# Attention and a four-layer gated FFN on one core: the operand differences of the two square layers go from GpSimd to VectorE, and the order of the work around them changes

## The chip, the cores and the metric

One core of a Trainium2 chip runs the whole kernel. The metric is the device time of one execution in microseconds, as the median over several runs; a run's profile is one execution more, with a time of its own.

## The reference, cut to what matters

H has 16 batches of 512 tokens by 256 features. Each is normalised; the result feeds a linear attention with 16 heads and a gated FFN with two square hidden layers of 1024, and all of it is added up.

```
xn  = layernorm(x)
# attention
q, k, v = split(xn @ W_qkv.T + b_qkv);  q, k = elu(q)+1, elu(k)+1
o   = (q @ (k.T @ v)) / clip(q . sum(k), 1e-6)          # per head
att = layernorm(o @ W_proj.T + b_proj) * gamma + beta + xn
# FFN, _tlin(x, w, s) = (x @ w.T) * s, w ternary
h   = silu(_tlin(xn, w1, s1)) * _tlin(xn, w2, s2)
h   = gelu(_tlin(h, h1, s))        # square, 1024 x 1024
h   = gelu(_tlin(h, h2, s))        # square, 1024 x 1024
out = x + att + _tlin(h, w3, s3)
```

## The kernel before, in words

A tile is one batch: 512 tokens. The loop runs over 16 tiles; the first has a body of its own (plain products, while the weights arrive), the next 14 are a loop, the last a copy of it without a successor. Each engine has one program, in order, written out by hand; engines meet at semaphores, which count named steps (`Count`, `Named`). A `Named` counter takes its value from the place of a name in a tuple, so the tuples `HI`, `LO` and `POOL_T` fix the order in which ScalarE, VectorE and GpSimd make their blocks.

The stages of a tile on PE are: eight gate groups (`gate_group`), with the attention's small products between them; the first square layer; the second square layer; the output groups with the projections of q, k and v of the next tile between them. The gate groups use a ring of three pairs of PSUM banks, so group n waits until VectorE has made the gated value of group n-3 (`gated`). The attention of this tile ends inside the first square layer: `to_rows` (transposes) and `proj_step`.

A square layer is computed by a scheme of seven products instead of eight (Winograd's form of Strassen). The operand's four blocks are B11, B12, B21, B22 (halves of the features by halves of the tokens), and the differences are T1 = B12-B11, T2 = B22-T1, T3 = B22-B12, T4 = B21-T2. Product i takes the block `X_OF[i]`: 1 B11, 5 T1, 6 T2, 7 T3, 2 B21, 3 B22, 4 T4, in this order. Output features are cut in four sets: sets 0 and 1 are the first layer, 2 and 3 the second; a step of `products(t, pair, i, parts)` computes product i of both sets of a layer. The operand of the first layer is in two groups G0 and G1, that of the second in H0 and H1.

Each operand is split for precision: `hi_of_block` and `hi_of_difference` on ScalarE write the high part as float32r, `lo` on VectorE (L1713) writes value x 4096 minus high as float16. A product takes the high parts and the low parts in two passes; `HI_FIRST` and `LO_FIRST` say which pass is first. The weights are ternary and exact in one part.

The partial sums of a layer are made by VectorE from the banks (`add_u`, `add_w`, `add_c22`, `add_c12`, `add_c21`, all L1739); `product_bank_read` is the wait of a product until its bank has been read. ScalarE applies the gelu (`gelu_of`).

GpSimd computes the differences (`t1` L756, `t2` L763, `t3` L768, `t4` L773), the roots of both LayerNorms (`inverse_root`, L746), and issues the refills of the weight ring. The ring holds seven blocks in four parts (`RING_PARTS`), and is filled four times a tile from DRAM (`refill`, L783): `refill(t, turn, g)` waits until the last product that reads part g in this turn is done, then loads that part for the next turn. SyncE loads the next x, stores the output, and loads six pieces of raw weights a tile (`load_piece`, L599), which VectorE inspects for bits that a shortened form would lose (`check_piece`, L1828); piece j+1 is requested when piece j has been inspected.

At the end of a tile VectorE adds gain, shift and sum of the attention's LayerNorm (`ln2_gain_and_shift`, `ln2_sum`), makes the low parts of the output operand (`lo_of_output`, L1720), reads the projections of the next tile (`z_step`, `phi_q`, `phi_k`) and writes the output halves (`output`). PE's `kv_step(t, c)` for c of 2 and 3 reuses the bank that `z_step(t, c-2)` has read.

Of the kernel before, what the change touches and what calls it, by code (L numbers as in the profile page):

```python
# [9 lines left out]
ALU = mybir.AluOpType  # L10
# [139 lines left out]
      "H0B11", "H1B11", "H0T1", "H1T1", "H0T2", "H1T2", "H0T3", "H1T3", "H0B22", "H1B22", "H0T4", "H1T4", "H0B21", "H1B21",  # L150
# [28 lines left out]
def block_kernel(nc, H, w_ffn, w_attn, vecs, rows, consts, out):  # L179
# [233 lines left out]
    pool_t = Named(sem("difference_made_by_pool"), POOL_T)  # L413
# [77 lines left out]
    def difference_made(t, group, block):  # L491
        return pool_t.after(t, group + block)
# [78 lines left out]
    with block:  # L571
# [163 lines left out]
        def _(pool):  # L735
# [18 lines left out]
            def t1(t, group):  # L754
                pool.wait_ge(*value_made(t, group, "B12"))
                tt(value(group, "T1"), value(group, "B12"), value(group, "B11"), ALU.subtract).then_inc(pool_t.sem, 1)  # L756

            def t2(t, group):
                pool.wait_ge(*value_made(t, group, "B22"))
                pool.wait_ge(*difference_made(t, group, "T1"))  # L760
                if group == "H1":
                    pool.wait_ge(*prod.after(t, "1P4"))
                tt(value(group, "T2"), value(group, "B22"), value(group, "T1"), ALU.subtract).then_inc(pool_t.sem, 1)  # L763

            def t3(t, group):
                pool.wait_ge(*value_made(t, group, "B22"))
                pool.wait_ge(*difference_made(t, group, "T1"))
                tt(value(group, "T3"), value(group, "B22"), value(group, "B12"), ALU.subtract).then_inc(pool_t.sem, 1)  # L768

            def t4(t, group):  # L770
                pool.wait_ge(*value_made(t, group, "B21"))
                pool.wait_ge(*lo_made(t, group, "T2"))
                tt(value(group, "T4"), value(group, "B21"), value(group, "T2"), ALU.subtract).then_inc(pool_t.sem, 1)  # L773

# [52 lines left out]
            def body_of(first):  # L827

                def body(t, more):
                    filling = first == 0  # L830
                    t1(t, "G0")
                    t2(t, "G0")
                    t4(t, "G0")
                    t3(t, "G0")
# [8 lines left out]
                    if filling:  # L843
                        refill(t, 0, 1)
                        refill(t, 0, 2)
# [1356 lines left out]
```

## Time and profile before

| | us |
|---|---|
| median of 3 runs | 1586.86 (1582.5 to 1591.64) |
| the profiled execution | 1580.62 |
| its span | 1578.7 |
| PE busy | 1485.9 (94%) |
| VectorE (DVE) busy | 1237.4 (78%) |
| ScalarE (ACT) busy | 927.2 (59%) |
| GpSimd (POOL) busy | 513.4 (33%) |
| DMA | 287.67 MB, 182 GB/s in the mean |

The profile is of one execution. Busy time is summed over an engine's instructions; PE's weight loads (PEld) overlap its matmuls. The first 126 us hold the first tile, then the same pattern of stages repeats tile after tile. Where an engine stood idle, the views name what released it.

### The profile page before, as it was taken

What the parts mean: (1) busy time and instruction counts of PE and PEld (TensorE: products, weight loads), DVE (VectorE), ACT (ScalarE), POOL (GpSimd) and SP (SyncE); (2) the same over time, 40 slices, a digit from 0 to 9 for tenths busy, and PEclk for the clock granted to TensorE, in tenths of its full rate; (3) what the DMA queues carried; (4) which work ended last, traced back from release to release, by engine and by line L of the source; (5) the groups of instructions that cost most, each with busy time, mean ns of one, the idle gap of its engine ahead of it and who ended that gap; (6) DMA issues with size and microseconds to landing.
All of it is one profiled execution on the core that took longest, in us unless ns stands there. A gap on an engine that the chain in (4) does not pass through costs nothing.

```text
span 1578.7 us, 33322 instructions
## 1 busy us (share of the span) xinstructions
PE 1485.9 (94%) x11020; PEld 1284.1 (81%) x11020; DVE 1237.4 (78%) x2088; ACT 927.2 (59%) x1727; POOL 513.4 (33%) x584
## 2 busy tenths in 40 slices
PE   9999999999999999999999998999999999999998
PEld 6998878788787887878878788788887878878887
DVE  6857878779687786877978779687786878968778
ACT  4545656556565565655666556565556656656564
POOL 2203415134151341513425034250342404424142
PEclk9999999999999999999999999999999999999999
DMA  8796726537165371653727438174481743817444
GB/s 234 232 318 214 280 70 223 199 102 282 62 222 200 103 280 64 224 198 117 263 67 252 170 132 287 39 251 160 132 285 44 256 159 129 287 39 263 152 146 151
DMA packets 89091, 287.67 MB, mean 182 GB/s; under 512 B 9696, under 2 KB 55392, under 8 KB 65760
## 3 DMA queue, kind: packets, MB, share of 16 engines
q0 software_dynamic: 43296, 231.75, 42.8%
q1 hardware_dynamic: 44928, 54.29, 10.5%
q10 hardware_dynamic: 832, 1.18, 0.2%
q8 instruction: 19, 0.31, 0.1%
q14 instruction: 16, 0.13, 0.0%
HBM read 270.42 MB, written 25.17 MB: 187 GB/s over the span
## 4 chain that ended last, share of the span: by engine, by line
PE 40%; issue 19%; DVE 14%; ACT 11%; POOL 8%; DMA 6%; DVEq 1%; POOLq 0%; ACTq 0%; SPq 0%
PE ps L1018 7%; PE ps L1016 6%; PE ps L1045 6%; DMA raw_weights<-weight_blocks 4%; PE ps L905 4%; PE ps L1132 4%; PE ps L1080 4%; PE ps L907 3%; PE ps L906 3%; DVE lo_a_in_bits L1713 3%; ACT values_out L1384 3%; POOL values_a L768 2%; DVE lo_b_in_bits L1713 2%; PE ps L957 2%; DVE attention_by_row L1693 2%
## 5 line engine op out<-in xcount | busy, mean ns | idle before, releaser
L1045 PE MATMUL ps<-operands_a,hidden_weights 128*128 128x256 f32 x2520 | 353.8, 284 | 0.0
L1045 PE MATMUL ps<-lo_a_in_bits,hidden_weights 128*128 128x256 f16 x2520 | 320.8, 273 | 0.0
L1045 PEld LDWEIGHTS ps<-operands_a,hidden_weights 128*128 128x128 f32 x2520 | 319.6, 189 | 0.5
L1045 PEld LDWEIGHTS ps<-lo_a_in_bits,hidden_weights 128*128 128x128 bf16 x2520 | 242.3, 98 | 30.0
L1713 DVE SCALAR_TENSOR_TENSOR lo_a_in_bits<-values_a,operands_a 128x512 f16<-128x512 f32 x315 | 231.4, 758 | 29.7 <-ACT operands_a L1356 18.3
L783 POOL DMA_DIRECT2D hidden_weights<-weight_blocks x236 | 131.8, 559 | 337.0 <-PE ps L1045 301.1
L756 POOL TENSOR_TENSOR values_a<-values_a 128x512 f32<-128x512 f32 x45 | 57.9, 1288 | 399.1 <-DVE values_a L1704 380.1
L1045 PE MATMUL ps<-operands_b,hidden_weights 128*128 128x256 f32 x840 | 140.1, 289 | 48.0 <-DMA hidden_weights<-weight_blocks 24.1
L1713 DVE SCALAR_TENSOR_TENSOR lo_b_in_bits<-values_b,operands_b 128x512 f16<-128x512 f32 x105 | 167.2, 1592 | 6.8 <-ACT operands_b L1356 6.4
L1045 PEld LDWEIGHTS ps<-operands_b,hidden_weights 128*128 128x128 f32 x840 | 114.0, 189 | 54.6 <-issue 51.8
L1356 ACT ACTIVATE operands_a<-values_a 128x512 fp32r<-128x512 f32 x180 | 113.3, 629 | 67.2 <-POOL values_a L756 26.5
L1018 PE MATMUL ps<-xnT,w_ffn 128*128 128x512 f32 x512 | 150.5, 421 | 0.0
L1648 DVE TENSOR_TENSOR zkv<-ps,row_vectors 128x512 f32<-128x512 f32 x64 | 44.2, 691 | 117.1 <-PE ps L907 116.9
L1739 DVE TENSOR_TENSOR partial_sums<-partial_sums,ps 128x512 f32<-128x512 f32 x150 | 102.3, 682 | 36.8 <-PE ps L1045 36.7
L1045 PE MATMUL ps<-lo_b_in_bits,hidden_weights 128*128 128x256 f16 x840 | 128.0, 275 | 0.1
L1310 ACT ACTIVATE gate_ring<-ps,vectors 128x512 f32<-128x512 f32 x128 | 86.1, 684 | 67.0 <-PE ps L1016 47.6
L1016 PE MATMUL ps<-xnT_lo_in_bits,w_ffn 128*128 128x512 f16 x512 | 124.6, 381 | 0.0
L1384 ACT ACTIVATE values_out<-partial_sums,vectors 128x256 f32<-128x256 f32 x90 | 40.9, 502 | 137.5 <-DVE partial_sums L1739 137.5
L1384 ACT ACTIVATE values_b<-partial_sums,vectors 128x256 f32<-128x256 f32 x90 | 40.8, 501 | 133.0 <-DVE partial_sums L1739 133.0
L1704 DVE SCALAR_TENSOR_TENSOR values_a<-ps,vectors,gate_ring 128x512 f32<-128x512 f32 x128 | 94.1, 745 | 30.0 <-ACT gate_ring L1310 29.9
L1018 PEld LDWEIGHTS ps<-xnT,w_ffn 128*128 128x128 f32 x512 | 93.1, 189 | 21.2
L1402 ACT ACTIVATE exp_tmp<-zkv 128x256 f32<-128x256 f32 x64 | 26.6, 416 | 123.6 <-DVE q L1642 67.2
(167 smaller groups left out, 2965.1 us busy)
## 6 DMA issues: line engine op xcount, KB each, us to landing
hidden_weights<-weight_blocks POOLq DMA_DIRECT2D x180, 1024.0 KB, 5.5
hidden_weights<-weight_blocks POOLq DMA_DIRECT2D x60, 512.0 KB, 5.1
raw_weights<-weight_blocks SPq DMA_DIRECT2D x70, 231.5 KB, 3.0
hidden_weights<-in_w_ffn POOLq DMA_DIRECT2D x16, 512.0 KB, 7.9
weight_blocks<-weight_sums SPq DMA_DIRECT2D x16, 512.0 KB, 4.8
weight_blocks<-in_w_ffn SPq DMA_DIRECT2D x16, 512.0 KB, 10.1
out_dram<-acc SPq DMA_DIRECT2D x31, 256.0 KB, 2.2
x<-in_H SPq DMA_DIRECT2D x15, 512.0 KB, 5.4
```

Of the source, the lines that this page charges most:

```text
L783: pool.dma_start(of_ring(ring, g), part_weights((turn + 1) % SETS, g)).then_inc(ring_loaded[g].sem, 16)
L905: mm(bank, wl, xh, start=first, stop=False)
L1016: r = mm(gate_bank(o, j), high_halves(wk), xnT_short[:, k, :], start=begins, stop=ends)
L1018: r = mm(gate_bank(o, j), wk, as_used(xnT[:, k, part, :]), start=begins, stop=ends)
L1045: r = mm(bank[:, m * HT:(m + 1) * HT], wk, xk, start=i in firsts and begins and m == 0 and j == 0, stop=i in lasts and ends and m == 1 and ...
L1080: r = mm(bank[:, m * HT:(m + 1) * HT], wk, parts[part][:, j, :], start=n < 4 and g == 0 and part == order[0] and m == 0 and j == 0, stop=n ...
L1310: nc.scalar.activation(gate[:, n % 2, :], gate_bank(o, 0), ACT.Silu, scale=vec[:, V_GATE + o:V_GATE + o + 1]).then_inc(silu_made.sem, 1)
L1356: nc.scalar.activation(hi_part(group, block), value(group, block), ACT.Copy, scale=LIFT).then_inc(hi.sem, 1)
L1384: r = nc.scalar.activation(dst, src[:, m * HT:(m + 1) * HT], ACT.Gelu, scale=vec[:, col:col + 1])
L1704: v.scalar_tensor_tensor(out=ha_values[:, o % HK, first:first + 2, 1, :], in0=two(gate_bank(o, 1)), scalar=vec[:, V_UP + o:V_UP + o + 1], ...
L1713: v.scalar_tensor_tensor(out=part, in0=value(group, block), scalar=LIFT, in1=hi_part(group, block).bitcast(F32), op0=ALU.mult, op1=ALU.sub ...
L1739: v.tensor_tensor(partial(s, dst), partial(s, kept), product_bank(s, i), ALU.add).then_inc(add.sem, 1)
```

## The change: what it does

The eight differences of each layer are computed by VectorE (`difference`, with `t1` to `t4` in its program), each once, with the same operands; the counter is renamed. GpSimd's program keeps the roots and the refills. Three refills more stand ahead of the LayerNorm 1 root (the four of turn 0, then parts 0 and 1 of turn 1), three between the roots (turn 1's parts 2 and 3, turn 2's part 0), and turn 2's part 1 stands behind the LayerNorm 2 root.

The orders change too. On PE the third product of the first layer runs before the row transposes, the fourth before the projection, and some steps swap their passes. On VectorE the sums of the first layer come before the rows' low part, `ln1_stats` and `ln2_stats` later, and in tiles with a successor `ln2_gain_and_shift` and `ln2_sum` move from before the first output block to behind the last. On ScalarE the exponentials of q go ahead of each last high part, and `residual` ahead of G1's T3.

```diff
@@ tuples
-POOL_T = ("G0T1", "G0T2", "G0T4", "G0T3", "G1T1", "G1T2", "G1T3", "G1T4",
-          "H0T1", "H1T1", "H0T2", "H1T2", "H0T3", "H1T3", "H0T4", "H1T4")
+DVE_T = ("G0T1", "G0T2", "G0T3", "G0T4", "G1T1", "G1T2", "G1T3", "G1T4", "H0T1", "H1T1", "H0T2", "H1T2", "H0T3", "H1T3", "H0T4", "H1T4")
@@ GpSimd, body: all t1..t4 removed, the rest in this order
                     if filling:
                         refill(t, 0, 0)
                         refill(t, 0, 1)
                         refill(t, 0, 2)
+                        refill(t, 0, 3)
+                        refill(t, 1, 0)
+                        refill(t, 1, 1)
                     if more:
                         ln1(t + 1)
                     if filling:
-                        refill(t, 0, 3)
-                        refill(t, 1, 0)
+                        refill(t, 1, 2)
+                        refill(t, 1, 3)
+                        refill(t, 2, 0)
                     inverse_root(t, 1, ln2_var, ln2_root)
                     if filling:
...
                         refill(t, 2, 1)
@@ PE, body
                     products(t, 0, 5, LO_FIRST)
+                    products(t, 0, 6, HI_FIRST)
                     to_rows(t, 0)
                     to_rows(t, 1)
-                    products(t, 0, 6, HI_FIRST)
+                    products(t, 0, 7, HI_FIRST)
                     proj_step(t, 0)
                     proj_step(t, 1)
-                    products(t, 0, 7, HI_FIRST)
-                    products(t, 0, 2, LO_FIRST)
-                    products(t, 0, 3, HI_FIRST)
-                    products(t, 0, 4, LO_FIRST)
-
-                    products(t, 1, 1, HI_FIRST)
-                    products(t, 1, 5, LO_FIRST)
-                    products(t, 1, 6, HI_FIRST)
+                    products(t, 0, 2, HI_FIRST)
+                    products(t, 0, 3, LO_FIRST)
+                    products(t, 0, 4, HI_FIRST)
+
+                    products(t, 1, 1, LO_FIRST)
+                    products(t, 1, 5, HI_FIRST)
+                    products(t, 1, 6, LO_FIRST)
@@ ScalarE, body
                 keep_first(t, 1)
+                residual(t)
                 hi_of_difference(t, "G1", "T3")
-                residual(t)
...
                 gelu_of(t, 3, "C21")
+                if more:
+                    q_act(t + 1, 0)
                 hi_of_output(t, 0, "C21")
+                if more:
+                    q_act(t + 1, 1)
                 hi_of_output(t, 1, "C21")
@@ VectorE
+            def difference(t, group, block, one, other):
+                v.tensor_tensor(value(group, block), value(group, one), value(group, other),
+                                ALU.subtract).then_inc(dve_t.sem, 1)
+            def t2(t, group):
+                if group == "H1":
+                    dve.wait_ge(*prod.after(t, "1P4"))
+                if group[0] == "G":
+                    dve.wait_ge(*value_made(t, group, "B22"))
+                dve.wait_ge(*difference_made(t, group, "T1"))
+                difference(t, group, "T2", "B22", "T1")
@@ VectorE, body, gate stage
                     cut_kv(t, 1)
+                    t1(t, "G0")
                     lo(t, "G0", "B11", first > 0)
+                    gated(t, 5)
                     lo(t, "G0", "T1", first > 0)
-                    gated(t, 5)
+                    t2(t, "G0")
                     normalise(t, 0)
                     gated(t, 2)
+                    t3(t, "G0")
                     lo(t, "G0", "T2", first > 0)
                     gated(t, 6)
+                    t4(t, "G0")
                     swap(t, 0)
                     gated(t, 3)
+                    t1(t, "G1")
                     lo(t, "G1", "B11", first > 0)
                     gated(t, 7)
+                    lo(t, "G1", "T1", first > 0)
+                    t2(t, "G1")
                     normalise(t, 1)
-                    lo(t, "G1", "T1", first > 0)
                     lo(t, "G0", "T3", first > 0)
                     lo(t, "G1", "T2", first > 0)
                     swap(t, 1)
+                    t3(t, "G1")
+                    t4(t, "G1")
@@ VectorE, body, second layer
                     add_c12(t, 0)
                     add_c12(t, 1)
+                    t1(t, "H0")
+                    t1(t, "H1")
+                    t2(t, "H0")
                     add_c21(t, 0)
                     add_c21(t, 1)
+                    t2(t, "H1")
 
                     lo(t, "H0", "T1", first > 0)
                     lo(t, "H1", "T1", first > 0)
                     lo(t, "H0", "T2", first > 0)
                     lo(t, "H1", "T2", first > 0)
+                    t3(t, "H0")
+                    t3(t, "H1")
+                    lo(t, "H0", "B22", first > 0)
+                    lo(t, "H1", "B22", first > 0)
+                    ln2_stats(t)
+                    lo(t, "H0", "T3", first > 0)
+                    lo(t, "H1", "T3", first > 0)
+                    add_u(t, 2)
+                    add_u(t, 3)
+                    t4(t, "H0")
+                    t4(t, "H1")
                     if checking and more:
                         check_piece(t - 1, 1)
@@ VectorE, body, end of the tile
-                    ln2_gain_and_shift(t)
-                    ln2_sum(t)
+                    if not more:
+                        ln2_gain_and_shift(t)
+                        ln2_sum(t)
...
                     lo_of_output(t, 0, "C21", first > 0)
                     lo_of_output(t, 1, "C21", first > 0)
                     if more:
+                        ln2_gain_and_shift(t)
+                        ln2_sum(t)
                         z_step(t + 1, 0)
                         output(t, 0)
```

## Rows read from the trace of the kernel before

**Rows 1.** The page, parts 1 and 2: busy time, granted clock in 40 slices.
```profile
PE 1485.9 (94%) x11020; PEld 1284.1 (81%) x11020; DVE 1237.4 (78%) x2088; ACT 927.2 (59%) x1727; POOL 513.4 (33%) x584
...
PEclk9999999999999999999999999999999999999999
```

**Rows 2.** Waits of PE, 810 to 907: total us, times, longest.
```profile
PE ps L905 <- ACT relu_tmp L1397: 1.8, 1, 1.8
PE ps L1045 <- DVE partial_sums L1739: 1.7, 1, 1.7
PE ps L1045 <- DMA hidden_weights<-weight_blocks: 1.7, 1, 1.7
PE ps L905 <- DVE attention_by_row L1693: 0.5, 1, 0.5
PE ps L1132 <- ACT hidden_out L1361: 0.4, 1, 0.4
```

**Rows 3.** Stages of one tile: us, busy us of each engine, clock, DMA, GB/s.
```profile
806.00:824.00 18.00, 18.00 (x97) 12.31 (x96) 13.78 (x29) 11.23 (x19) 5.10 (x4) 1.00 0.09 28
...
854.00:867.00 13.00, 11.28 (x99) 10.52 (x98) 12.60 (x8) 9.96 (x20) 11.38 (x12) 1.00 0.90 334
...
884.00:903.00 19.00, 16.81 (x106) 13.92 (x105) 12.12 (x21) 10.79 (x22) 0.53 (x1) 1.00 0.37 126
```

**Rows 4.** Timeline of DVE, 850 to 870: start, us, instruction, idle before.
```profile
855.16 4.09 DVE L1713 SCALAR_TENSOR_TENSOR lo_b_in_bits<-values_b,operands_b 128x512 f16<-128x512 f32 x1
...
859.77 3.53 DVE L1713 SCALAR_TENSOR_TENSOR lo_b_in_bits<-values_b,operands_b 128x512 f16<-128x512 f32 x1
...
863.83 1.78 DVE L1828 SCALAR_TENSOR_TENSOR low_bits<-raw_weights,low_bits 128x463 uint32<-128x463 uint32 x1
865.53 1.76 DVE L1713 SCALAR_TENSOR_TENSOR lo_b_in_bits<-values_b,operands_b 128x512 f16<-128x512 f32 x1
```

**Rows 5.** Timeline of POOL, 840 to 867.
```profile
840.93 1.04 POOL L746 TENSOR_TENSOR rstd<-var_plus_eps,power 128x4 f32<-128x4 f32 x1 [4.52 <-DVE minus_mean L1597]
...
849.81 1.43 POOL L746 TENSOR_TENSOR rstd<-var_plus_eps,power 128x4 f32<-128x4 f32 x1 [5.32 <-DVE minus_mean L1597]
...
851.90 1.15 POOL L783 DMA_DIRECT2D hidden_weights<-weight_blocks  x2 [0.38 <-issue]
...
857.40 1.29 POOL L763 TENSOR_TENSOR values_a<-values_a 128x512 f32<-128x512 f32 x1
...
865.04 1.70 POOL L773 TENSOR_TENSOR values_a<-values_a 128x512 f32<-128x512 f32 x1
```

**Rows 6.** Groups of DVE by form: count, busy us, mean ns, idle before.
```profile
L1797 DVE TENSOR_TENSOR acc<-acc,partial_sums 128x512 f32<-128x512 f32 x31 | 21.5, 693 | 2.3
...
L1777 DVE TENSOR_TENSOR projected<-projected,row_vectors 128x1024 f32<-128x1024 f32 x16 | 19.5, 1219 | 0.0
```

**Rows 7.** Timeline of DVE, gate stage.
```profile
815.21 0.29 DVE L1664 TENSOR_TENSOR kv_by_head<-ps,constants 128x128 f32<-128x128 f32 x1 [1.14 <-PE ps L957]
...
822.36 0.75 DVE L1704 SCALAR_TENSOR_TENSOR values_a<-ps,vectors,gate_ring 128x512 f32<-128x512 f32 x1 [0.32 <-ACT gate_ring L1310]
```

**Rows 8.** Timeline of ACT at the end of the gate stage.
```profile
823.15 0.63 ACT L1343 ACTIVATE operands_a<-values_a 128x512 fp32r<-128x512 f32 x1 [0.30 <-DVE values_a L1704]
```

**Rows 9.** Timeline of PE, products of both square layers and the next gate stage.
```profile
824.01 2.13 PE L1045 MATMUL ps<-operands_a,hidden_weights 128*128 128x256 f32 x16
...
841.42 3.67 PE L1045 MATMUL ps<-lo_a_in_bits,hidden_weights 128*128 128x256 f16 x32
...
869.82 0.74 PE L1045 MATMUL ps<-operands_b,hidden_weights 128*128 128x256 f32 x4 [1.75 <-DVE partial_sums L1739]
...
903.14 1.10 PE L1018 MATMUL ps<-xnT,w_ffn 128*128 128x512 f32 x4
```

**Rows 10.** Landing of the check pieces, 806 to 904 (line L599).
```profile
DMA to landing us min/median/max: 1.7/2.8/5.3
```

**Rows 11.** Landing of the ring's refills, whole span (line L783).
```profile
DMA to landing us min/median/max: 3.4/5.2/8.1
```

More of the change, by code:

```diff
@@ L491, in difference_made @@
     def difference_made(t, group, block):
-        return pool_t.after(t, group + block)
+        return dve_t.after(t, group + block)
     def value_made(t, group, block):
@@ L1734, in plain_lo_of_output, with t1, t3, t4 @@
                                        op1=ALU.subtract).then_inc(plain_lo.sem, 1)
+            def difference(t, group, block, one, other):
+                v.tensor_tensor(value(group, block), value(group, one), value(group, other),
+                                ALU.subtract).then_inc(dve_t.sem, 1)
+            def t1(t, group):
+                dve.wait_ge(*value_made(t, group, "B12"))
+                difference(t, group, "T1", "B12", "B11")
+            def t2(t, group):
[5 more added lines that the diff above has]
+                difference(t, group, "T2", "B22", "T1")
+            def t3(t, group):
+                dve.wait_ge(*difference_made(t, group, "T1"))
+                difference(t, group, "T3", "B22", "B12")
+            def t4(t, group):
+                dve.wait_ge(*value_made(t, group, "B21"))
+                dve.wait_ge(*lo_made(t, group, "T2"))
+                difference(t, group, "T4", "B21", "T2")
             def sum_into(t, s, i, dst, kept):
@@ L2049, in body @@
                     lo(t, "G1", "B21", first > 0)
+                    add_u(t, 0)
+                    add_u(t, 1)
                     rows_lo(t, 0)
                     rows_lo(t, 1)
-                    add_u(t, 0)
-                    add_u(t, 1)
                     lo(t, "G0", "B22", first > 0)
                     lo(t, "G1", "B22", first > 0)
-                    if more:
-                        ln1_stats(t + 1)
                     add_w(t, 0)
@@ L2063, in body @@
                     lo(t, "G1", "T4", first > 0)
-                    ln2_stats(t)
+                    if more:
+                        ln1_stats(t + 1)
+                    lo(t, "H0", "B11", first > 0)
+                    lo(t, "H1", "B11", first > 0)
                     if checking and more:
@@ L2068, in body @@
                     add_c12(t, 1)
-                    lo(t, "H0", "B11", first > 0)
-                    lo(t, "H1", "B11", first > 0)
+                    t1(t, "H0")
+                    t1(t, "H1")
+                    t2(t, "H0")
                     add_c21(t, 0)
                     add_c21(t, 1)
+                    t2(t, "H1")
                     lo(t, "H0", "T1", first > 0)
@@ L2113, in body @@
                     lo_of_output(t, 1, "C11", first > 0)
+                    lo_of_output(t, 0, "C12", first > 0)
+                    lo_of_output(t, 1, "C12", first > 0)
                     add_c21(t, 2)
                     add_c21(t, 3)
-                    lo_of_output(t, 0, "C12", first > 0)
-                    lo_of_output(t, 1, "C12", first > 0)
                     if checking and more:
```

56 lines of the change are left out of this document (2 added, 54 removed).

## The prediction

> **What bounds the kernel now.** The page first: PE is busy 94% of the span at the full clock, so PE can only be given back its waits [rows 1]. Its timeline repeats every 97.1 us, once a tile. I take the tile whose gate groups begin at 806.0; its successor's begin at 903.14 [rows 9]. PE's waits in it are five and add up to 6.1 us: 0.5 for the projection's rows, 1.7 for a refill, 1.7 for VectorE's sums, 0.4 for the output operand, 1.8 for q's exponentials [rows 2]. Then the stages: in 854 to 867 VectorE is busy 12.60 of 13 us and GpSimd 11.38; in the gate stage and in the tail both have room [rows 3]. The timelines of the two say why. Three low halves of H0 take 4.09, 3.53 and 1.76 us and a check piece 1.78, where the usual is 0.68 and 0.64, and the first ends 0.5 us after a pair of GpSimd subtractions does (858.69), the last 0.5 us after one that ends at 866.74 [rows 4, 5]. The excess is 3.4+2.85+1.1+1.1 = 8.5 us a tile. The 1.7 us until 869.82 is this backlog: product 7 waits for the sum of set 2 [rows 9]. The 1.7 us for the DMA begins at GpSimd: it sits in the LayerNorm 2 root until 851.5 and only then, at 851.90, issues the refill of part 1, freed at 846.8; it lands 5.1 us later [rows 5].
>
> The Trainium skill (SBUF — State Buffer, Who interferes with whom) says that a VectorE instruction with two SBUF inputs and a GpSimd instruction that reads SBUF exclude each other, the second waiting for the first. By that rule too the stretch goes with the subtractions.
>
> **The change part by part,** on that tile's clock.
>
> *The subtractions.* 16 leave GpSimd (1.29 us each) and join VectorE. This form is not on VectorE now; the nearest rows are 512 columns from two SBUF tiles in 0.69 us and 1024 in 1.22, so 512 more columns cost 0.53 and an instruction in a row about 0.60 [rows 6]. I take 0.60, 9.6 us a tile (bounds 0.53 and 0.69: 8.5 to 11). The removed stretch is 8.5 (bounds 0, if it stays, and 8.5). VectorE's total stays near 79 us a period; what counts is where the work stands.
>
> *Gate stage (six of them before the products).* VectorE has gaps up to 815.2. From there chained: cut 0.35, T1 0.6, low B11 0.6, gated 5 0.65, low T1 0.6, T2 0.6, normalisation 1.7, gated 2 0.65, T3 0.6, low T2 0.6, gated 6 0.65, T4 0.6, swap 0.7: 8.9 us, so gated 3 starts at 824.1, not 822.36 [rows 7]. G1's first high half on ScalarE, at 823.15 now, comes at 824.9 to 825.5 [rows 8]. Product 1 starts at 824.01 and needs it after its first quarter of 0.5 us [rows 9]: **a new PE wait of 1.1**. The gate groups' banks are free in time (gated 2 ends at 821.0, the last group starts at 821.2: 0.2 of slack). Later in this layer: low T1 of G1 is made at 828.0 and wanted at 829.3, low T2 at 831.5 and 834.5, the rows' low part at 839.8, before the projection at 840.8, because product 7 now runs ahead of it: the 0.5 wait goes. The layer with projection ends at 854.7 (now 854.1).
>
> *Refill wait.* Part 1 of turn 1 is issued ahead of the roots, when product 2 ends at 847.4, and lands at 852.7: the 1.7 goes. Its cover is 2 us; were GpSimd held up by more, it would return.
>
> *Second layer.* VectorE: sums C12 at 852.7 (product 3 ends at 851.0), ScalarE's gelu of C12 853.0 and 853.8, T1s 853.7 and 854.5, T2 of H0 855.1, sums C21 856.3, T2 of H1 856.9, low T1s 858.1, low T2s 859.4 (on ScalarE's high halves), T3s 860.6, low B22s 861.8, LayerNorm 2 statistics 3.3 us to 865.1, low T3s 866.3, sum of set 2 866.9. PE has products 1, 5, 6 without a wait, 3 times 3.67, and the transposes 0.9: 854.7 to 866.6 [rows 9]. **Wait 0.4** for the sum, where 1.7 was. But the root now stands before the refill of part 1, turn 2: statistics 865.1, issue 2.2 later (as 849.7 to 851.9), landing 5.1 later: 872.4 [rows 5, 11]. PE wants it at 870.7: **a new wait of 1.7** (bounds 0 and 4.6, from the landings of 3.4 and 8.1). Still product 2 starts 1.2 ahead of its 873.6 now. Behind it stands the check: piece 1 is inspected at 869.3, not 865.6, so piece 2 is asked for with three refills in flight and lands after 2.8 to 5.3 us [rows 10]. VectorE waits there, in order, until 872.6 or 874.9, and behind it stand the sums that free product 3's bank: **0 to 1.2**. I take half, 0.6. The products end at 883.9 (now 884.5).
>
> *Tail.* q's exponentials go ahead of a high half: the 1.8 shrinks to 0.2, and out_group's 0.4 goes, its operand being a microsecond ahead. But the last low half comes 1.3 us later in ScalarE's row (the second half's exponentials lie before it), and behind it VectorE has gain, shift and sum, 3 times 1.22 and gaps, 3.75 us [rows 6], before the first z. Chained: last low half 893.6, sum 897.4, z0 898.0, output 899.5, z1 900.1. PE wants z0 at 897.7 and z1 at 899.4: **0.3 and 0.7**. The next gate stage starts at 901.8 (bounds 901.3 and 902.2 by the piece's landing): 1.3 us a tile, 0.9 to 1.8. The balance says the same: 6.1 leave; 1.1+0.4+1.7+0.6+0.2+0.3+0.7 = 5.0 come; between 1.1 and 1.3.
>
> *At nothing.* The swapped passes leave the number of changes between float32 and float16 matmuls as it is. ln1_stats stands 6 us later; its root is wanted at 861 and done by 850. residual ahead of G1's T3: that high half is made at 834.0, wanted at 837.6. No SyncE instruction moves; the output's store still has 24 us until residual.
>
> **Sum.** 14 tiles with a successor at 1.3, the last 0.8: 19 us. The profiled execution took 1580.6 us (span 1578.7 and 1.9 around it): 1561.6. The median of the three runs is 1586.9, 0.4% above that execution; 1586.9-19 = 1568, say 1567.
>
> The same section of the Trainium skill (SBUF — State Buffer) speaks against the change too: GpSimd's roots read SBUF, and VectorE's many two-input instructions may hold them off. The power took 1.04 us in one place and 1.43 in the other [rows 5], so this case shows 0.4. By the rule each of the roots' short instructions could wait for one of VectorE's, 0.6; the sum would be at most 1.2 us a tile worse, 17 in all.
>
> **Rivals.**
> A, more (chance 0.21): the piece lands in 2.8 us, the refill in 3.4. 2.5 to 3.5 us a tile: 1535 to 1550. For it: SyncE's pieces land in under 3 us as a rule. Against: three refills in flight.
> B, nothing (0.16): 1579 to 1594. Five new waits hang on one in-order VectorE; a quarter microsecond more in each eats the 1.3.
> C, slower (0.16): the turn of the tile is bound by VectorE. z, output, phi and gated 0 stand in one row behind the 3.75 us; each microsecond by which that row is later than I have it moves kv_step, the gate stage and G1's high half one for one. It decides from 1.3 us a tile; at 2.5 the price is 1.2 x 15 = 18: 1605. For it: there is nothing in the row to drop. Against: VectorE is busy 12.12 of 19 us in that tail [rows 3].
> D, the stretch comes from the refills' issue, not the subtractions (0.03): 8.5 stays and 4.8 of subtractions come on top in the second layer; PE waits 4 us a tile more: 1645. Against: two refills are issued between 873 and 875 and nothing is stretched there.
> The forecast has 0.44, with an own range of 1555 to 1579.
>
> 0.5% (8 us) is what a measurement of this kernel can tell from no change. Faster 0.44+0.21 = 0.65, same 0.16, slower 0.16+0.03 = 0.19. The range 1538 to 1597 leaves out A's best end, D and C's far part.
>
> **What would show it.** Low halves of H0 at 0.68 us throughout; VectorE's busy time within 20 us of 1237, GpSimd's down by some 300; no DMA wait at the second layer's first product, one of about 1.7 at its product 2; about 1.1 for ScalarE's high half in the first product; two below 1 at kv_step; a period near 95.8. Wrong if the halves stay stretched, if PE waits in the gate groups, or if the period is over 96.7.

## The result, and the profile after

The changed kernel takes 1604.95 us (median, 1602.9 to 1606.0) against 1588.3 for the kernel before: ratio 1.0103, 95% interval 1.008 to 1.0125. It is slower by 1%, where I forecast 1567 and gave "slower" 0.19. The profiled execution took 1602.9 us, 22 more than that of before.

The page of the changed kernel, parts 1 and 2:

```profile
PE 1494.5 (93%) x11020; PEld 1290.0 (81%) x11020; DVE 1243.2 (78%) x2328; ACT 925.1 (58%) x1727; POOL 207.7 (13%) x344
...
PEclk9999999999999999999999999999999999999999
```

VectorE's busy time is within 6 us of what it was, as forecast, and GpSimd's fell by 306 us [rows 1]. The stretch is gone: groups by form of the changed kernel, the low halves of H0 and the subtractions (count, busy us, mean ns, idle before).

```profile
L1695 DVE TENSOR_TENSOR values_a<-values_a 128x512 f32<-128x512 f32 x180 | 121.4, 681 | 2.1
...
L1670 DVE SCALAR_TENSOR_TENSOR lo_b_in_bits<-values_b,operands_b 128x512 f16<-128x512 f32 x105 | 71.9, 684 | 43.1 <-ACT operands_b L1298 43.0
```

0.684 us where the mean was 1.59. A subtraction takes 0.68 by itself and its successor starts 0.60 us later, which is the cost that I took. So the idea of the change works, and the time is lost elsewhere. Who PE waits for in one tile of the changed kernel, 813 to 912 (total us, times, longest), the rows that answer to [rows 2]:

```profile
PE ps L1000 <- DVE partial_sums L1723: 4.0, 2, 3.6
PE ps L1000 <- DMA hidden_weights<-weight_blocks: 1.7, 1, 1.7
PE ps L1000 <- ACT operands_a L1298: 0.6, 1, 0.6
PE ps L860 <- ACT relu_tmp L1352: 0.6, 1, 0.6
PE ps L860 <- DVE zkv L1605: 0.5, 2, 0.4
```

7.4 us instead of 6.1. Each is one that the prediction named; one has another size. The timeline of PE in that tile:

```profile
874.52 0.74 PE L1000 MATMUL ps<-operands_b,hidden_weights 128*128 128x256 f32 x4 [0.47 <-DVE partial_sums L1723]
...
880.10 0.61 PE L1000 MATMUL ps<-lo_b_in_bits,hidden_weights 128*128 128x256 f16 x4 [1.66 <-DMA hidden_weights<-weight_blocks]
...
887.47 0.74 PE L1000 MATMUL ps<-operands_b,hidden_weights 128*128 128x256 f32 x4 [3.56 <-DVE partial_sums L1723]
...
902.13 0.50 PE L860 MATMUL ps<-wqkv_parts,xnT 128*128 128x512 f32 x1 [0.56 <-ACT relu_tmp L1352]
...
909.41 0.50 PE L860 MATMUL ps<-wqkv_parts,xnT 128*128 128x512 f32 x1 [0.17 <-DVE zkv L1605]
...
911.42 0.50 PE L860 MATMUL ps<-wqkv_parts,xnT 128*128 128x512 f32 x1 [0.35 <-DVE zkv L1605]
...
912.92 1.10 PE L973 MATMUL ps<-xnT,w_ffn 128*128 128x512 f32 x4
```

0.47 for the sum of set 2 (forecast 0.4), 1.66 for the refill behind the root (1.7), 0.56 for the exponentials (0.2), 0.17 and 0.35 for z (0.3 and 0.7), and at the first product 0.59 for ScalarE's high half (1.1). And 3.56 us at product 3, where I had 0.6. The tile starts at 813.79 and the next at 912.92: 99.1 us, where I said 95.8 and 97.1 was. (Of the 2.0 us more only 1.3 stand in these rows. Most of the other 0.7 shows when starts are compared instead of idle times: each wait puts the next start off by 0.16 to 0.24 us more than its row says, there are seven waits in place of five, and one of 0.2 at 903.84 has no row.) What VectorE does ahead of the sums that PE waits for, its timeline:

```profile
876.11 0.63 DVE L1812 SCALAR_TENSOR_TENSOR low_bits<-raw_weights,low_bits 128x463 uint32<-128x463 uint32 x1
...
884.31 0.64 DVE L1812 SCALAR_TENSOR_TENSOR low_bits<-raw_weights,low_bits 128x463 uint32<-128x463 uint32 x1 [4.56 <-DMA raw_weights<-weight_blocks]
884.86 0.68 DVE L1587 SCALAR_TENSOR_TENSOR xnT<-ps,xnT 128x512 fp32r<-128x512 f32 x1
885.47 0.68 DVE L1723 TENSOR_TENSOR partial_sums<-partial_sums,ps 128x512 f32<-128x512 f32 x1
```

It stands 4.56 us in front of check piece 2. Four sums follow (885.47 to 887.9), and the third of them frees PE's bank. GpSimd and SyncE say why the piece is late, their timelines:

```profile
857.16 0.74 POOL L747 TENSOR_TENSOR minus_mean_by_rstd<-minus_mean,rstd 128x4 f32<-128x4 f32 x1
...
872.68 1.40 POOL L745 TENSOR_TENSOR rstd<-var_plus_eps,power 128x4 f32<-128x4 f32 x1 [6.65 <-DVE minus_mean L1554]
874.16 0.20 POOL L747 TENSOR_TENSOR minus_mean_by_rstd<-minus_mean,rstd 128x4 f32<-128x4 f32 x1
874.74 1.15 POOL L761 DMA_DIRECT2D hidden_weights<-weight_blocks  x2 [0.38 <-issue]
878.14 0.53 POOL L761 DMA_DIRECT2D hidden_weights<-weight_blocks  x1 [2.25 <-PE ps L1000]
879.04 0.53 POOL L761 DMA_DIRECT2D hidden_weights<-weight_blocks  x1 [0.37 <-issue]
```

```profile
876.90 0.34 SPq L598 DMA_DIRECT2D raw_weights<-weight_blocks  x1
```

The LayerNorm 2 root ends at 874.4 and lets two refills go at once, two more follow at 878.14 and 879.04, 3.5 MB in all. Piece 2 is asked for at 876.90 in the middle of them and lands after 7.3 us, at 884.21. The four refills land at 879.9, 882.7, 885.5 and 886.7, so the piece lands behind the two that were asked for before it and ahead of the two behind it. The landings over six tiles, first of the kernel before, then of the changed one (line of the check pieces):

```profile
DMA to landing us min/median/max: 1.5/2.7/5.7
```

```profile
DMA to landing us min/median/max: 1.8/2.6/7.4
```

One thing more is in the records: the granted clock of PE. It stands at one of two levels, full (2.4 GHz) or half (1.2 GHz); a stretch at half, which lasts 3.4 or 6.8 us here, is called a fall below. Its mean over the profiled execution is 0.983 where it was 0.989. That is a difference between two executions and not between the kernels: over their executions the changed kernel shows 0.979 to 0.983, and the kernel before 0.977 to 0.984 in the 26 that ran beside e1 to e8.

### The profile page after: what moved, and what is told of

Its sections match the earlier page's. It is cut to its first block, busy times and chain, and to the rows that moved or that the text cites. A ratio compares the mean times of both kernels' runs of the same rounds, so it can differ in the third digit from the quotient of the medians.

```text
span 1601.1 us, 33162 instructions
## 1 busy us (share of the span) xinstructions
PE 1494.5 (93%) x11020; PEld 1290.0 (81%) x11020; DVE 1243.2 (78%) x2328; ACT 925.1 (58%) x1727; POOL 207.7 (13%) x344
## 4 chain that ended last, share of the span: by engine, by line
PE 43%; DVE 22%; issue 12%; ACT 11%; DMA 10%; DVEq 2%; SPq 0%; ACTq 0%
PE ps L1000 20%; DMA raw_weights<-weight_blocks 10%; PE ps L973 4%; PE ps L971 4%; PE ps L1035 3%; DVE partial_sums L1723 3%; ACT values_a L1339 3%; DVE values_a L1695 3%; DVE lo_a_in_bits L1670 2%; PE ps L860 2%; PE ps L862 2%; PE ps L861 2%; ACT values_out L1339 2%; PE ps L912 2%; PE ps L1087 2%
## 5 line engine op out<-in xcount | busy, mean ns | idle before, releaser
L1000 PE MATMUL ps<-operands_a,hidden_weights 128*128 128x256 f32 x2520 | 361.0, 287 | 8.9 <-ACT operands_a L1298 8.9
L1000 PEld LDWEIGHTS ps<-operands_a,hidden_weights 128*128 128x128 f32 x2520 | 327.7, 193 | 12.3 <-ACT operands_a L1298 12.0
L1670 DVE SCALAR_TENSOR_TENSOR lo_a_in_bits<-values_a,operands_a 128x512 f16<-128x512 f32 x315 | 209.0, 683 | 13.5 <-ACT operands_a L1311 13.5
L1000 PE MATMUL ps<-operands_b,hidden_weights 128*128 128x256 f32 x840 | 150.2, 303 | 58.5 <-DVE partial_sums L1723 58.5
L1000 PEld LDWEIGHTS ps<-operands_b,hidden_weights 128*128 128x128 f32 x840 | 121.0, 201 | 65.4 <-issue 61.0
L1677 DVE SCALAR_TENSOR_TENSOR lo_out_in_bits<-values_out,hidden_out 128x512 f16<-128x512 f32 x120 | 78.6, 687 | 78.8 <-ACT hidden_out L1316 78.8
L1812 DVE SCALAR_TENSOR_TENSOR low_bits<-raw_weights,low_bits 128x463 uint32<-128x463 uint32 x84 | 53.3, 634 | 98.9 <-DMA raw_weights<-weight_blocks 98.9
L1695 DVE TENSOR_TENSOR values_a<-values_a 128x512 f32<-128x512 f32 x180 | 121.4, 681 | 2.1
L1000 PEld LDWEIGHTS ps<-lo_b_in_bits,hidden_weights 128*128 128x128 bf16 x840 | 79.5, 101 | 39.9 <-DVE lo_a_in_bits L1670 15.3
L1670 DVE SCALAR_TENSOR_TENSOR lo_b_in_bits<-values_b,operands_b 128x512 f16<-128x512 f32 x105 | 71.9, 684 | 43.1 <-ACT operands_b L1298 43.0
```

Source lines behind the costliest of these rows:

```text
L1000: r = mm(bank[:, m * HT:(m + 1) * HT], wk, xk, start=i in firsts and begins and m == 0 and j == 0, stop=i in lasts and ends and m == 1 and ...
L1670: v.scalar_tensor_tensor(out=part, in0=value(group, block), scalar=LIFT, in1=hi_part(group, block).bitcast(F32), op0=ALU.mult, op1=ALU.sub ...
L1677: v.scalar_tensor_tensor(out=part, in0=hg_values[p][:, :, O_SLOT[c], 1, :], scalar=LIFT, in1=hg[p][:, :, O_SLOT[c], 0, :].bitcast(F32), op ...
L1695: v.tensor_tensor(value(group, block), value(group, one), value(group, other), ALU.subtract).then_inc(dve_t.sem, 1)
```

## The experiments

The *period* below is the mean distance, over 14 tiles of the profiled execution, between ScalarE's loads of the silu table, one a tile: 97.85 us before, 99.37 after. "Clock" is the mean granted clock of PE in the profiled execution.

| kernel | median us | ratio to before (95%) | period | clock |
|---|---|---|---|---|
| before | 1588 to 1591 | 1 | 97.85 | 0.989 |
| changed | 1604.95 | 1.0103 (1.008 to 1.0125) | 99.37 | 0.983 |
| e1 check early | 1542.96 | 0.9695 (0.9679 to 0.9711) | 95.09 | 0.998 |
| e2 refill early | 1542.27 | 0.9692 (0.9676 to 0.9709) | 95.03 | 0.998 |
| e3 both | 1531.0 | 0.9625 (0.9609 to 0.9641) | 94.18 | 0.999 |
| e4 piece 2 behind the sums | 1600.95 | 1.0068 (1.0051 to 1.0085) | 99.16 | 0.988 |
| e5 no pieces | 1526.88 | 0.9604 (0.9585 to 0.9623) | 93.94 | 1.000 |
| e6 before, check late | 1591.3 | 1.0012 (0.9997 to 1.0027) | 98.67 | 0.984 |
| e7 e3, differences on GpSimd | 1570.85 | 0.9881 (0.9861 to 0.99) | 97.49 | 0.991 |
| e8 e3, ballast | 1594.56 | 1.0035 (1.0024 to 1.0046) | 99.07 | 0.970 |
| e9 tuned | 1507.97 | 0.9505 (0.9474 to 0.9535) | 92.68 | 1.000 |
| e10 before, root later | 1586.77 | 0.9993 (0.9974 to 1.0012) | 98.44 | 0.975 |

**e1_check_early.**

```diff
                     lo(t, "H1", "T2", first > 0)
+                    if checking and more:
+                        check_piece(t - 1, 1)
                     t3(t, "H0")
...
                     t4(t, "H1")
-                    if checking and more:
-                        check_piece(t - 1, 1)
```

> One edit to the changed kernel: VectorE inspects raw piece 1 right after the low T2s of the second layer (where the kernel before had it), not after both T4s. Theory Q (queue): the changed kernel is slow because piece 2 is asked for some 8 us later than before, at the moment when the LayerNorm 2 root has let four refills go at once; it lands 7.3 us later and VectorE stands in front of the sums that free product 3's bank (PE's 3.56 us). Asked for 7 us earlier it lands before the backlog: that PE wait goes, period 99.1 to about 95.6, time 1602.9 - 14 x 3.5 = 1554 (1550 to 1565). Rival L (load): the sums are late because VectorE now carries 16 subtractions; then the wait only changes its name and under 1 us a tile comes back: 1590 to 1603.

Measured: 1543, 62 us faster than the changed kernel and 7 below the low end of what I expected. One instruction of VectorE's row for a tile moved up, and nothing else. Piece 2 is now asked for 9.2 us earlier in the tile and lands in about 3 us. (The expectation has the changed kernel ask for it 8 us later than the kernel before; in the tiles shown it is 3.3.) PE's waits in one of its tiles, 780 to 875:

```profile
PE ps L1000 <- DMA hidden_weights<-weight_blocks: 1.6, 1, 1.6
PE ps L1000 <- DVE partial_sums L1723: 1.1, 1, 1.1
PE ps L1000 <- ACT operands_a L1298: 0.6, 1, 0.6
PE ps L860 <- DVE zkv L1605: 0.5, 2, 0.3
```

The sums cost 1.1 instead of 4.0. VectorE runs the same 2328 instructions, so rival L falls.

**e2_refill_early.**

```diff
                         refill(t, 2, 0)
+                        refill(t, 2, 1)
                     inverse_root(t, 1, ln2_var, ln2_root)
                     if filling:
-                        refill(t, 2, 1)
```

> One edit to the changed kernel: GpSimd issues the refill of part 1, turn 2, ahead of the LayerNorm 2 root. Theory Q: PE's DMA wait of 1.66 us goes for certain, and the backlog is spread, so piece 2 lands in 3 to 5 us instead of 7.3 and half or more of the 3.56 goes too: 3 us a tile, 1561 (1550 to 1578). Rival L: only the DMA wait goes, and PE meets the late sums 1.7 us earlier, so the wait for them grows by as much: 1595 to 1603.

Measured: 1542, 8 us below the low end of what I expected. The DMA wait is gone from the rows, and the wait for sums fell to 1.65 a tile (13.2 in eight), although piece 2 is asked for at the same place of the tile as in the changed kernel. It lands in 3.5 to 3.8 us. The late request needs the backlog to do harm.

**e3_both_early.** Both edits.

> Both edits together: piece 1 inspected early and the refill of part 1, turn 2, ahead of the root. Theory Q: both waits go, 1.66 + 3.5 = 5.2 us a tile less, 1602.9 - 14 x 5.2 = 1530; a part comes back at the next late thing (the sum of set 2, the last low half, z), so 1532 to 1545. Rival L: 1585 to 1600. If the two edits cure the same wait, e3 is no faster than the better of the two alone.

Measured: 1531, 1 us below the low end. The two cure one wait between them and 1.7 us of another: together 74 us, singly 62 and 63. Waits of PE in one tile, 758 to 852:

```profile
PE ps L1000 <- DVE partial_sums L1723: 1.3, 2, 1.0
...
PE ps L860 <- DVE zkv L1605: 0.5, 2, 0.3
```

**e4_piece2_behind_sums.**

```diff
-                    if checking and more:
-                        check_piece(t - 1, 2)
                     if more:
                         transposed_lo(t + 1, 1)
...
                     add_c22(t, 3)
+                    if checking and more:
+                        check_piece(t - 1, 2)
                     if more:
                         cut_lo(t + 1)
```

> One edit to the changed kernel: the inspection of piece 2 stands behind the sums that free the banks (after add_c22 of set 3), the late request stays as it is. Theory Q with the in-order row as the means: the piece still lands after about 7 us, but nobody behind it is wanted by PE, so PE's 3.56 us goes; piece 3 is asked for no earlier and is met again before the first output block: 2.5 to 3.5 us a tile, 1554 to 1568. If instead the DMA backlog hurts PE by itself (the refills, not the piece), the wait stays: 1600.

Measured: 1601, only 4 us faster: my expectation of 1554 to 1568 failed. The wait for the sums is gone, as said, and another has its place, in PE's timeline:

```profile
895.32 1.21 PE L1087 MATMUL ps<-w_out,hidden_out 128*128 128x256 f32 x8 [2.00 <-ACT hidden_out L1316]
...
901.60 0.69 PE L860 MATMUL ps<-wqkv_parts,xnT 128*128 128x512 f32 x1 [2.27 <-ACT relu_tmp L1352]
```

Piece 3 is requested only when piece 2 has been inspected, and it stands ahead of the first output block. VectorE waits in this kernel as long for pieces as in the changed one (100.6 us over the span against 98.9), and PE pays at the output operand and at the exponentials instead of at product 3. The pieces are a chain: request, landing, inspection. Moving one inspection back moved the place where the chain is met, not the time that it takes. So the wait is the chain's, not the sums'.

**e5_no_pieces.** SyncE loads no pieces in the loop, VectorE does not wait for them (its six instructions work on its own low bits): this part of the inspection is left out.

```diff
             def load_piece(turn, j):
+                return
...
-                dve.wait_ge(piece_loaded[j].sem, piece_loaded[j].at(turn, 0))
-                v.scalar_tensor_tensor(out=low[:], in0=raw[:], scalar=0xFFFF, in1=low[:],
+                v.scalar_tensor_tensor(out=low[:], in0=low[:], scalar=0xFFFF, in1=low[:],
```

> The changed kernel, but the raw weight pieces are neither loaded nor waited for in the loop (VectorE still runs the six instructions, on its own low bits), so this part of the inspection is left out; the refills and their order stay. Theory Q: all of PE's 3.56 us goes, as in e1, the refill's 1.66 stays, DMA has 1.6 MB less a tile: 1540 (1532 to 1547). If the refills' backlog or VectorE's load were the cause the wait would stay near 3 us: over 1585.

Measured: 1527, 5 us below the low end. The refill's wait is still there, and the wait for sums is 0.5 a tile. PE's waits over eight tiles, 600 to 1400:

```profile
PE ps L1000 <- DMA hidden_weights<-weight_blocks: 13.1, 8, 1.8
...
PE ps L1000 <- DVE partial_sums L1723: 4.1, 8, 0.5
```

So the refills' backlog alone does PE no more harm than the 1.6 us. The rest came by the pieces.

**e6_before_late_check.** The same move of the inspection as e1 undoes, made in the kernel before.

```diff
                     lo(t, "H1", "T2", first > 0)
-                    if checking and more:
-                        check_piece(t - 1, 1)
...
                     add_u(t, 3)
+                    if checking and more:
+                        check_piece(t - 1, 1)
```

> The kernel before, with one edit: VectorE inspects piece 1 after the sums of product 6 (set 3) instead of before the low T3s, 5 us later. If lateness alone makes the 7 us landing, the tile gets 2 us longer or more: 1620. Theory Q (late request together with a backlog let go by the root): there is no root ahead of these refills here, piece 2 lands in 3 to 5 us and meets VectorE at or shortly before its turn: 0 to 0.7 us a tile, 1590 to 1600.

Measured: 1591, ratio 1.0012 and not to be told from no change. Piece 2 is asked for 62 to 64 us behind the tile's load of the silu table, later than in the changed kernel (61), and lands in 2.5 to 3.2 us, not in 7.3: a late request is not enough, it has to meet the refills. It is not free either, in PE's waits over eight tiles, 600 to 1400, first of the kernel before, then of e6:

```profile
PE ps L1045 <- DVE partial_sums L1739: 12.4, 8, 2.0
PE ps L1132 <- ACT hidden_out L1361: 3.7, 7, 0.8
```

```profile
PE ps L1132 <- ACT hidden_out L1361: 12.5, 8, 1.8
PE ps L1045 <- DVE partial_sums L1739: 5.5, 8, 0.9
```

The wait for the sums shrinks, and a wait for the output operand takes its place; the two about cancel.

**e7_e3_differences_on_gpsimd.** e3 with `t1` to `t4` on GpSimd (before's functions, in the gaps of e3's refills, so the refills and roots keep e3's order) and none on VectorE.

> e3 (both waits cured, 94.1 us a tile) with all sixteen subtractions back on GpSimd, the other orders as in e3: what the move itself is worth. My reading of the stretch: the low halves of H0 take 3 to 4 us again, 8.5 us a tile, the sum of set 2 is late by 2 to 3 us; in the gate stage 1.1 us comes back because VectorE has no subtractions there. 2 to 3.5 us a tile more than e3, with falls of the clock 1575 to 1600. If the stretch costs PE nothing: 1520 to 1531.

Measured: 1571, 4 us below the low end. The move of the sixteen subtractions is worth 40 us by the medians, 2.8 a tile (3.3 between the profiled executions; that of e7 is 5 us above its median). A part of it is the clock, which falls to half in eight of e7's 14 tiles and in none of e3's. The low halves are stretched again, here in both buffers, the longest to 5.8 us; groups by form:

```profile
L1718 DVE SCALAR_TENSOR_TENSOR lo_a_in_bits<-values_a,operands_a 128x512 f16<-128x512 f32 x315 | 278.2, 902 | 60.1 <-ACT operands_a L1359 47.7 <-ACT operands_a L1346 10.4
...
L1718 DVE SCALAR_TENSOR_TENSOR lo_b_in_bits<-values_b,operands_b 128x512 f16<-128x512 f32 x105 | 95.4, 909 | 62.6 <-ACT operands_b L1346 42.6 <-ACT operands_b L1359 20.0
```

And the orders of the change without the move of the subtractions, once repaired, are worth 18 us against the kernel before.

**e8_e3_ballast.**

```diff
                         transposed_lo(t + 1, 1)
+                        for _ in range(6):
+                            dve.drain()
+                            v.tensor_reduce(spare[:], rowv[:, 0:N], AX_X, ALU.max)
                     add_w(t, 2)
```

> e3 with six idle reductions (512 columns, 0.6 us each, 3.7 us in all) on VectorE ahead of the sums that free product 3's bank: the PE wait of 3.6 us of the changed kernel, without any late piece or backlog. By the wait alone: 14 x 3.5 = 49 us over e3's 1531, 1580, and the granted clock stays 0.998. If a PE wait of this length also makes the chip take the clock down, as the records of the changed kernel suggest (0.983 there, 0.998 in e1 to e3): falls of 3.4 us at half speed in most tiles, another 15 to 25 us: 1595 to 1605, clock 0.98.

Measured: 1594.6, clock 0.970. PE's wait is 4.81 us here, not 3.6, since the six reductions with their drains take 4.5 us and not 3.7. Timeline of PE, and stretches around the wait (us, busy us of each engine, clock, DMA share, GB/s):

```profile
687.67 1.21 PE L1001 MATMUL ps<-operands_b,hidden_weights 128*128 128x256 f32 x4 [4.81 <-DVE partial_sums L1724]
```

```profile
682.00:684.00 2.00, 0.86 (x8) 0.66 (x6) 1.83 (x3) 0.00 (x0) 0.53 (x1) 1.00 1.05 406
684.00:686.00 2.00, 0.00 (x0) 0.00 (x0) 1.85 (x4) 0.00 (x0) 0.00 (x0) 0.80 1.08 303
686.00:688.00 2.00, 0.33 (x1) 0.34 (x2) 2.00 (x4) 0.43 (x2) 0.00 (x0) 0.50 1.03 406
688.00:690.00 2.00, 2.00 (x11) 2.00 (x11) 1.29 (x3) 2.00 (x7) 0.00 (x0) 0.50 0.07 25
...
692.00:694.00 2.00, 2.00 (x20) 1.79 (x19) 1.68 (x3) 1.37 (x4) 0.00 (x0) 1.00 0.00 0
```

PE is idle from 682.9 to 687.7. The granted clock is full at first, falls to half about 2 us into the wait and stays there until 692, so PE works 4 us at half speed (11 matmuls in 2 us where 20 is usual). This comes in each of the 14 tiles of e8 and in none of e3, which differs only by the ballast: this wait brings the clock down, and no late piece is needed for it. What the half speed costs in time is less than I had in my upper case: e8's period is 4.9 above e3's, of which 4.0 stand in the rows of waits. That leaves at most 0.9 a tile, 13 us in all.

**e9_tuned.** e3 with three orders of VectorE changed.

```diff
                     t4(t, "G0")
-                    swap(t, 0)
                     gated(t, 3)
+                    swap(t, 0)
...
+                    add_u(t, 2)
+                    add_u(t, 3)
                     lo(t, "H0", "T3", first > 0)
                     lo(t, "H1", "T3", first > 0)
-                    add_u(t, 2)
-                    add_u(t, 3)
...
                         put_ones(t + 1)
+                        ln2_gain_and_shift(t)
+                        ln2_sum(t)
                     lo_of_output(t, 0, "C21", first > 0)
                     lo_of_output(t, 1, "C21", first > 0)
                     if more:
-                        ln2_gain_and_shift(t)
-                        ln2_sum(t)
                         z_step(t + 1, 0)
```

> e3 with three orders of VectorE's row changed: the swap of the attention's first half stands behind gated 3 (G1's high half 0.65 us earlier, PE's 0.59 at the first product goes); the sums of product 6 of sets 2 and 3 stand ahead of the low T3s (1.2 us earlier, PE's 1.04 goes); gain, shift and sum stand ahead of the low halves of C21, in the 3.7 us in which VectorE waits for ScalarE there (z 3.7 us earlier, PE's two waits of 0.5 in all go). If the waits are what e3 still loses: 2.1 to 2.3 us a tile, 94.1 to 91.9, 1531 - 31 = 1500 (1496 to 1508). Rival: the row is full and each order only moves the wait to the next product (the low T3s, the additions of product 5): 1520 to 1530.

Measured: 1508, the top end of what I expected (1496 to 1508). It is 5.0% faster than the kernel before (0.9505, 0.9474 to 0.9535) and 6% faster than the changed one. PE's waits over eight tiles, 600 to 1400:

```profile
PE ps L1000 <- DVE lo_b_in_bits L1670: 9.4, 9, 1.0
PE ps L1000 <- DVE partial_sums L1723: 2.1, 9, 0.2
```

2.5 us a tile of e3's waits went, 1.4 came back at the next things in VectorE's row (11.5 us in eight tiles, most of it at a low half of H0), partly as the rival had it. The period fell by 1.5. The three orders were changed together; what each is worth by itself is not shown.

**e10_before_root_later.**

```diff
                         refill(t, 1, 0)
+                        refill(t, 1, 1)
                     inverse_root(t, 1, ln2_var, ln2_root)
                     if filling:
-                        refill(t, 1, 1)
```

> The kernel before, with one edit: GpSimd issues the refill of part 1, turn 1, ahead of the LayerNorm 2 root instead of behind it. If a root in front of a refill is what PE waits for at 856.96, that 1.7 us goes; what follows in the second layer is bound by VectorE's stretched low halves, so PE meets the sum of set 2 earlier and waits longer there: 0.5 to 1.5 us a tile, 1567 to 1581. If the landing is bound by the DMA engines and not by the issue, nothing: 1588.

Measured: 1586.8, no change, outside my 1567 to 1581. The DMA wait went, so the root was its cause, but PE then meets the stretched low halves, in its timeline:

```profile
859.68 0.61 PE L1045 MATMUL ps<-lo_b_in_bits,hidden_weights 128*128 128x256 f16 x4 [0.83 <-DVE lo_b_in_bits L1713]
862.70 1.03 PE L1045 MATMUL ps<-lo_a_in_bits,hidden_weights 128*128 128x256 f16 x4 [2.41 <-DVE lo_a_in_bits L1713]
```

0.8+2.4 in place of 1.7+1.7. In the kernel before, the stretch stood right behind the refill as the next bound of that stage. That PE gained nothing is not all the stretch's doing, though: behind these two waits the clock is at half for 6.8 us in eight of the 14 tiles, where the falls of the kernel before last 3.4, and the two can't be told apart here. e7 against e3 is the cleaner test of the stretch.

## Why the prediction was wrong

*The stretch and the subtractions:* right. 0.684 us for each low half and 0.68 for each subtraction, rival D refuted: of 145 low halves and subtractions that overlap the issue of a refill in the changed kernel, none took more than 0.70 us. e7 gives the move's price.

*Gate stage:* right in kind, wait 0.59 instead of 1.1. Gated 3 starts 17.9 us after the gate groups do (831.66 after 813.79), and I had 18.1; the groups' banks are free in time.

*First refill wait, second layer:* right; product 1 does not wait, and the sum of set 2 costs 0.47 where I had 0.4. *Root ahead of the refill:* right to 0.04 us. That order did more harm than its wait, as e2 shows.

*The check piece:* this is the step that failed. The prediction has it as "**0 to 1.2**. I take half, 0.6", from a landing of 2.8 to 5.3 us. It lands after 7.3 and PE waits 3.56. The mechanism was named, its size was read from the wrong place: the largest landing in a tile of before (5.3) was taken as the bound, though I had worked out myself that the root would hold the refill behind it back. There was a row for an estimate: 334 GB/s at a DMA share of 0.90 [rows 3], so 1 MB takes about 3 us, and 3.5 MB asked for around the piece keep the engines full for some 10. In the changed kernel they are full at 406 to 422 GB/s, and the four refills and the piece are through in about 11 us, from 876 until 886.7. Three refills overlapped the flight of the piece that took 5.3; four overlap that of 7.3. e1, e2 and e5 take the piece's lateness away in three different ways and each gives 60 us or more back. The DMA's stretches, with its share and GB/s in the last two columns:

```profile
876.00:878.00 2.00, 2.00 (x20) 1.81 (x19) 2.00 (x5) 2.00 (x5) 0.00 (x0) 1.00 0.95 287
878.00:880.00 2.00, 0.44 (x4) 0.14 (x2) 1.75 (x3) 1.78 (x4) 1.05 (x2) 1.00 1.06 422
880.00:882.00 2.00, 1.90 (x18) 1.74 (x19) 0.00 (x0) 0.00 (x0) 0.00 (x0) 1.00 1.04 407
...
884.00:886.00 2.00, 0.00 (x0) 0.00 (x0) 1.69 (x3) 0.00 (x0) 0.53 (x1) 1.00 1.08 406
```

*Tail:* right in kind and size (1.1 together, forecast 1.2).

*The sum:* PE's row for the piece is 3.0 us above my 0.6 in 13 tiles and 1.7 above it in the 14th, some 41 us, and 1561.6+41 comes within a microsecond of the measured 1602.9. That is luck. The piece costs more than its row. A tile of e1 takes 95.2 us and the tile shown 99.1, both at full clock throughout: 3.9 us, of which 3.8 are at product 3 by the starts and 0.8 at the exponentials, with 0.7 given back at product 7 and the refill. In the mean over the first 13 of the 14 tiles (the last is shorter in every kernel) it is 4.4: 99.6 against 95.2. So the step was short by 3.8 us a tile. What makes up for it is that the kernel before takes 98.1 in this mean and not the 97.1 of the tile that I read, a microsecond of clock that e1 does not lose. 3.8 - 1.0 = 2.8 a tile are 39 us, and the last tile adds 3, being 2 us longer where I had 0.8 less. Without the piece's wait the forecast of the period is good to 0.1: 95.8 less the 0.6 is 95.2, as in e1. There too single terms cancel: 0.6 for 1.1 in the gate stage, 1.05 for 0.4 at the sum of set 2, 0.5 for 1.2 in the tail.

*What was in no step:* the clock. The prediction has PE "at the full clock" from the slices of the page [rows 1], where a 9 stands for 0.9 and more and hides short falls. The time at the lower clock, twice (1 - mean clock) times the span, was 35 us of before's execution and 53 us of the changed kernel's. In the kernel before it is at half in nine of the 14 tiles; tiles without a fall take 97.0 to 97.3 us and those with one of 3.4 us 98.2 to 98.8, so a fall costs 1.1 to 1.6. In the changed kernel 11 of the 14 have one, but no such price can be read: they take 98.6 to 100.4, and of the three without one two take 99.1 and 99.8. So the clock does not explain why the changed kernel is slower than the kernel before, the more so as their clocks agree over the executions. It is a part of what the repairs gain: e1, e2, e3, e5 and e9 have no fall in these 14 tiles. Of the 60 us between the profiled executions of e1 and the changed kernel 14 x 3.9 = 55 come at full clock, which leaves about 5 for it.

*The rivals:* B, D and the forecast's own range are out. A's main condition, a piece that lands in 2.8 us, is about what e1 (3) and e2 (3.5 to 3.8) bring about, and they measured 1543 and 1542, in its range of 1535 to 1550. C ended on the right side and near the right time (1605) for another reason. VectorE's row decided the tile, but what made it late was a wait for a DMA inside it, at product 3, not gain, shift and sum in the tail: PE's two waits for z are 0.5 us in all, and they go in e9, which moves these three ahead.

The rule of the Trainium skill that I set against the change (SBUF — State Buffer, Who interferes with whom) is seen as well: the LayerNorm 1 root's second instruction took 0.74 us at 857.16, while VectorE made a low half from two SBUF tiles, and that of LayerNorm 2 took 0.20 at 874.16, beside sums with one operand in PSUM (`ps`). It is so in all 14 tiles, 0.61 to 0.74 against 0.20. The first root's price lies off the path. It changed nothing here.

What stays open is which waits bring the clock down. e8's of 4.8 us does it in all 14 tiles. Of the 14 of 3.5 us in the changed kernel 12 do, and that of the tile shown is one of the two that do not. e4 has a wait of 2.0 to 2.6 us in 12 tiles, in 11 of them with another of 0.7 to 2.3 within 7 us, and a fall in nine of the 12. The kernel before, with none above 2.1 us, has falls in nine tiles, and e1, with 1.1 and 1.5 to 1.8 us, in none of its 14. So the length of the wait alone does not decide it.

## What to carry to other kernels

When a transfer is requested later, read its landing from what will be in flight then: add up the bytes that are asked for around it, by the rate of a busy stretch, as an upper bound, and don't take the largest landing of the old schedule for it. A short instruction that waits in a queue which also issues DMAs can hold them back and then release them together; putting one refill ahead of it gave 62 us here (e2), and nothing where another wait stood right behind (e10). In an engine's in-order row every wait for a DMA stands in front of all that others need from it; inspect such rows for what has slack (the subtractions) and what has none (a chain of request, landing, inspection). And take the clock from its mean and from the tiles' lengths, not from the digits of a page: one tile without a fall is not the mean tile.

## What the runs showed of the hardware

VectorE instructions with two SBUF inputs were stretched from 0.68 to up to 4.1 us beside GpSimd subtractions (5.8 in e7), and never beside GpSimd's issues of refills.

In the tile shown, a small transfer that SyncE asked for in the middle of four refills took 7.3 us where the median of its kind is 2.6 (7.2 to 7.4 in 13 of the 14 tiles), and landed behind the two refills asked for before it and ahead of the two behind it.

A wait of PE can have a second price. After those of 3.5 us in the changed kernel, in 12 of 14 cases, and of 4.8 us in e8, in all, the granted clock is at half for 3.4 to 6.8 us, in which each 2 us hold about 11 matmuls instead of 20. What it adds to a tile was 1.1 to 1.6 us in the kernel before and at most 0.9 in e8. In the 14 tiles of e9 no wait is above 1.04 us, the clock is full over the whole span, and every one of them takes 92.64 to 92.75 us, where tiles of before differ by 2.
